# First attention of a two-layer transformer: head outputs closed up by transfers and their sums inverted once per half batch, instead of transposed on TensorE

## The reference

```
q, k, v = split(lora_linear(xn, ...))          # 16 heads of 16
attn = softmax(q k^T / 4)                      # per head, 1024 x 1024
s = lora_linear(concat_heads(attn v), Wo, ...)
x = x + s * g
...
quantize(w) = clip(round(w / (mean|w| + 1e-8)), -1, 1)
hidden = sigmoid(xn quantize(w1)^T) * (xn quantize(w2)^T)   # 704 wide
g = silu(hidden quantize(w3)^T)
```

## Time and profile before

| what | us |
|---|---|
| median of 3 runs | 3152.13 (3145.29 to 3154.65) |
| the profiled execution, its own time | 3151.62 |
| its span in the trace | 3149.8 |
| TensorE busy | 3008.4 (96%) |
| VectorE busy | 2125.9 (67%) |
| ScalarE busy | 1862.8 (59%) |
| first attention, from its first matmul to its last addition | 678.6 to 1450.2 |
| gate network, its first hidden matmul | 1471.3 |

### The profile page before, as it was taken

The page is one execution under the profiler, slowest core; times in us unless marked ns, Lnnn a source line. Parts: engine busy times, 40 slices in busy tenths (PEclk is TensorE's granted clock), DMA queues, the critical chain, the costliest instruction groups (busy, mean ns, idle before and its releaser), DMA issues. The chain is left out here.

```text
span 3149.8 us, 66397 instructions
## 1 busy us (share of the span) xinstructions
PE 3008.4 (96%) x23634; PEld 2263.1 (72%) x23634; DVE 2125.9 (67%) x5893; ACT 1862.8 (59%) x4638; POOL 994.0 (32%) x1611
## 2 busy tenths in 40 slices
PE   7999999999999999996988999999999999999998
PEld 5888888854444444434877888788887888788886
DVE  5666666679989999875755555655556555565556
ACT  4666666647877778783445555455554555545553
POOL 0000000000000000002016666576655766566663
PEclk9999999989999999998999999999999999999999
DMA  4111111232233133102324444354343443244432
GB/s 150 48 48 48 48 48 41 61 69 37 58 50 70 29 75 47 29 9 86 132 67 107 103 97 95 99 126 103 87 114 88 116 103 93 66 116 109 102 87 69
DMA packets 296708, 246.35 MB, mean 78 GB/s; under 512 B 149181, under 2 KB 231741, under 8 KB 296253
## 3 DMA queue, kind: packets, MB, share of 16 engines
q1 hardware_dynamic: 296380, 242.11, 31.6%
HBM read 100.71 MB, written 44.04 MB: 46 GB/s over the span
## 5 line engine op out<-in xcount | busy, mean ns | idle before, releaser
L1821 ACT ACTIVATE b_pp<-b_pp,b_nm 128x192 f32<-128x192 f32 (+2 forms) x1024 | 472.9, 463 | 447.7 <-DVE b_nm L1988 366.2
L973 ACT ACTIVATE a_pt<-ps 128x512 f32<-128x512 f32 x1024 | 555.9, 595 | 177.7 <-PE ps L1005 176.7
L176 DVE TENSOR_REDUCE mx<-ps 128x2 f32<-128x1024 f32 x512 | 622.5, 1224 | 55.5 <-PE ps L167 41.8
L1791 POOL TENSOR_SCALAR b_pp<-b_pp,b_rc 128x192 f32<-128x192 f32 x960 | 387.0, 425 | 386.3 <-DVE b_rc L1997 386.3
L2009 DVE COPY b_pt<-ps 128x384 f32<-128x384 f32 (+2 forms) x336 | 182.1, 556 | 317.9 <-PE ps L1910 302.6
L1988 DVE CUSTOM_DVE_ANT_0 b_pp<-ps,b_mk 128x192 f32<-128x192 f32 x960 | 276.3, 353 | 134.3 <-PE ps L1889 134.3
L800 DVE SCALAR_TENSOR_TENSOR f_yac<-ps,f_cw,f_yac 128x128 f32<-128x128 f32 x992 | 278.0, 344 | 125.4 <-PE ps L599 123.0
L958 POOL TENSOR_TENSOR a_s<-a_s,g 128x256 f32<-128x256 f32 x32 | 23.3, 729 | 880.6 <-DVE a_s L1069 880.6
L599 PEld LDWEIGHTS ps<-w,f_sq 128*128 128x128 f32 x2048 | 265.1, 191 | 26.5 <-issue 6.0
L599 PE MATMUL ps<-w,f_sq 128*128 128x128 f32 x2048 | 270.1, 275 | 0.3
L1944 PE MATMUL ps<-b_wo,b_oT 128*128 128x256 f32 x1024 | 241.6, 380 | 3.7 <-ACT b_vv L1814 3.7
(11 more groups left out here) (273 smaller groups left out, 7313.6 us busy)
## 6 DMA issues: line engine op xcount, KB each, us to landing
b_rt<-b_qf SPq DMA_DIRECT2D x1024, 64.0 KB, 2.0
qk_parts<-f_aa SPq DMA_DIRECT2D x32, 512.0 KB, 2.7
v_rows<-f_va_ SPq DMA_DIRECT2D x16, 512.0 KB, 2.8
rl<-in_W1qT SPq DMA_DIRECT2D x64, 128.0 KB, 2.6
rl<-in_W1kT SPq DMA_DIRECT2D x64, 128.0 KB, 2.7
rl<-in_W1vT SPq DMA_DIRECT2D x32, 256.0 KB, 3.3
b_wo<-in_W1oT SPq DMA_DIRECT2D x16, 512.0 KB, 4.0
b_vs<-b_vv SPq DMA_DIRECT2D x60, 128.0 KB, 2.8
```

The lines of the kernel that those rows point to most:

```text
L176: e.tensor_reduce(M["mx"][kh % 3][:, :, jt, h], P.pair(s), AX.X, ALU.max, negate=True).then_inc(P.free_sem(s), 1)
L973: e.activation(pt[(4 * i + 2 * j + a) % 12][:, :], P.ap((*s, a)), ACT.Exp).then_inc(P.free_sem((*s, a)), 1)
L1791: m = e.tensor_scalar(x, x, r[:, 2 * u + h:2 * u + h + 1], 1.0, ALU.mult, ALU.mult)
L1821: e.activation(x, x, ACT.Exp, bias=nm[n % 4][:, c:c + 1], scale=-1.0, accum_out=sm[n % 4][:, c:c + 1]).then_inc(exp_done, 1)
```

## The change

In the first attention the steps "one" and "two" are gone. After each evacuation SyncE sends eight transfers from SBUF to SBUF: for each of the 4 heads its 16 rows into a tile `oc` without gaps (line 977 of the new program), and its row of sums, folded to 8 rows of 64, into a tile `sm` (line 979). So all sums of a half batch (16 heads, 512 queries) stand in one 128 x 64 tile. Seven side steps per half batch follow: "invert", one reciprocal on VectorE; "spread", SyncE writes it to DRAM (line 983); "return", 16 transfers read it back, each head's row to 16 partitions (line 988); "x", two loads of 256 tokens (992); "norm", POOL multiplies `oc` in place in two parts; and "three" twice, now 256 tokens each, with four matmuls straight from `oc` (line 1097). Side steps still go to chunks 2 to 5; in the last half unit to chunks 1 to 7. The absolute sum and the rounding of w1 and w2 move from the gate network into units 1 and 2 of the first attention (load on SyncE, line 960; absolute sum on ScalarE; matmul; rounding in three passes on POOL). The rounding of w3 moves behind the first hidden step of the second chunk, and the memsets of that block go from VectorE to POOL.

```diff
+GATE = [(s, m, 16 + 20 * m + at) for m in range(2) for s, at in (("load", 0), ("size", 6), ("sum", 8), ("round", 9))]
...
+        p += [("weights", s, m) for s, m, at in GATE if at == i]
...
-        if 2 <= c <= 5 and side:
-            p.append(side.pop(0))
+        if side and (2 <= c <= 5 or c and i >= 16 * units - 8):
+            p += side.pop(0)
         p += ahead(2 * i + 2)
...
-                    p += side
-                    side = [("last",)]
-                f0 = 8 * (u // 4) + 4 * h
-                for n in range(6):
-                    side += [(s, f0 + n - lag) for lag, s in ((2, "three"), (1, "two"), (0, "one")) if 0 <= n - lag < 4]
-    return p + side
+                    p += [s for x in side for s in x]
+                    side = [[("last",)]]
+                f = u // 4 * 2 + h
+                side += [[("invert", f)], [("spread", f)], [("return", f)], [("x", 2 * f), ("x", 2 * f + 1)],
+                         [("norm", f)], [("three", 2 * f)], [("three", 2 * f + 1)]]
+    return p + [s for x in side for s in x]
 
...
+                elif s[:2] == ("weights", "load"):
+                    w.wait_ge(rounded, 3 * n)
+                    w.wait_ge(gate_set, 2)
+                    e.dma_start(raw[:, :, :], A[("f1T", "f2T")[n]].rearrange("(c p) o -> p c o",
+                                                                               p=128)).then_inc(raw_in, 16)
...
-                elif k == "one":
-                    w.wait_ge(x1_ready, n - 2)
-                    e.dma_start(xb[n % 3][:, :], A["x"][n * 128:(n + 1) * 128, :]).then_inc(xb_in[n % 3], 16)
+                elif k == "evac":
+                    b, g, h = n // 8, n // 2 % 4, n % 2
+                    x, f = op[n % 4], 2 * b + h
+                    w.wait_ge(*P.emptied(("group", n)))
+                    if f >= 4:
+                        w.wait_ge(*P.filled(("three", 2 * (f - 4) + 1)))
+                    for j in range(4):
+                        r = 64 * (g % 2) + 16 * j
+                        e.dma_start(oc[f % 4][r:r + 16, g // 2, :], x[32 * j:32 * j + 16, :]).then_inc(closed[n % 4], 16)
+                        r = 32 * g + 8 * j
+                        e.dma_start(sm[f % 4][r:r + 8, :], x[32 * j + 16:32 * j + 17, :].rearrange(
+                            "a (t q) -> a t q", q=64)).then_inc(closed[n % 4], 16)
+                elif k == "spread":
+                    w.wait_ge(rc_ready, n + 1)
+                    e.dma_start(X["inv"][n].rearrange("h (t q) -> (h t) q", q=64), rc[n % 2][:, :]).then_inc(rc_out, 16)
+                elif k == "return":
+                    w.wait_ge(rc_out, 16 * (n + 1))
+                    w.wait_ge(normed, 2 * n)
+                    for i in range(H0):
+                        e.dma_start(rb[i % 8 * 16:i % 8 * 16 + 16, i // 8, :],
+                                    X["inv"][n, i, :].partition_broadcast(16)).then_inc(rb_in, 16)
+                elif k == "x":
+                    w.wait_ge(x1_ready, n - 1)
+                    e.dma_start(xb[n % 2][:, :, :], A["x"][n * 256:(n + 1) * 256, :].rearrange(
+                        "(i p) d -> p i d", p=128)).then_inc(xb_in[n % 2], 16)
...
+                if k == "norm":
+                    w.wait_ge(rb_in, 256 * (n + 1))
+                    for g in (2, 3):
+                        w.wait_ge(*is_closed(8 * (n // 2) + 2 * g + n % 2))
+                    for m in range(2):
+                        x = oc[n % 4][:, :, 256 * m:256 * m + 256]
+                        e.tensor_tensor(x, x, rb[:, :, 256 * m:256 * m + 256], ALU.mult).then_inc(normed, 1)
...
+                elif s[:2] == ("weights", "size"):
+                    w.wait_ge(raw_in, 16 * (n + 1))
+                    e.activation(M["fq"][n][:, :, 0:FF], raw[:, :, :], ACT.Abs,
+                                 accum_out=size[:, n:n + 1]).then_inc(size_ready, 1)
                 elif k == "evac":
-                    u, h = n // 2, n % 2
-                    b, g = u // 4, u % 4
                     w.wait_ge(pv_done, pv_at[8 * n + 7, 1])
-                    if b >= 2:
-                        w.wait_ge(*P.filled(("one", 8 * (b - 2) + 7)))
-                    e.activation(oT[b % 2][:, g, h * CH:(h + 1) * CH], P.ap(("group", n)),
-                                 ACT.Copy).then_inc(P.free_sem(("group", n)), 1)
+                    if n >= 4:
+                        w.wait_ge(*is_closed(n - 4))
+                    e.activation(op[n % 4][:, :], P.ap(("group", n)), ACT.Copy).then_inc(P.free_sem(("group", n)), 1)
...
-                elif k == "one":
-                    b, t = n // 8, n % 8
-                    w.wait_ge(*P.emptied(("group", 2 * (4 * b + 3) + t // 4)))
-                    for g in range(4):
-                        m = e.transpose(P.ap(s)[:, g * 128:(g + 1) * 128], oT[b % 2][:, g, t * 128:(t + 1) * 128],
-                                        ident[:, :])
-                    m.then_inc(P.full_sem(s), 1)
-                elif k == "two":
-                    w.wait_ge(*P.emptied(("one", n)))
+                elif s[:2] == ("weights", "sum"):
+                    w.wait_ge(size_ready, n + 1)
+                    e.matmul(P.ap(s)[:, 0:3], ones[:, :], size[:, :], start=True, stop=True).then_inc(P.full_sem(s), 1)
+                elif k == "three":
+                    w.wait_ge(normed, n + 1)
                     for i in range(2):
-                        m = e.transpose(P.ap(s)[:, i * 128:(i + 1) * 128], av[n % 2][:, i * 128:(i + 1) * 128],
-                                        ident[:, :])
-                    m.then_inc(P.full_sem(s), 1)
-                elif k == "three":
-                    w.wait_ge(*P.emptied(("two", n)))
-                    for i in range(2):
-                        m = e.matmul(P.ap(s)[:, 0:256], aT[n % 2][:, i, :], M["wo"][:, i, :], start=i == 0,
-                                     stop=i == 1)
+                        t = slice(256 * (n % 2) + 128 * i, 256 * (n % 2) + 128 * i + 128)
+                        for j in range(2):
+                            m = e.matmul(P.ap(s)[:, i * 256:(i + 1) * 256], oc[n // 2 % 4][:, j, t], M["wo"][:, j, :],
+                                         start=j == 0, stop=j == 1)
...
-                elif k == "one":
-                    p = P.ap(s).rearrange("p (h r) -> p h r", r=32)
+                elif s[:2] == ("weights", "sum"):
                     w.wait_ge(*P.filled(s))
+                    e.tensor_scalar(thr[:, 0, n:n + 1], P.ap(s)[:, n:n + 1], 1.0 / (FF * D), 1e-8, ALU.mult,
+                                    ALU.add).then_inc(P.free_sem(s), 1)
+                elif k == "invert":
+                    for g in (2, 3):
+                        w.wait_ge(*is_closed(8 * (n // 2) + 2 * g + n % 2))
                     if n >= 2:
-                        w.wait_ge(*P.filled(("two", n - 2)))
-                    e.reciprocal(rc[n % 2][:, :], p[:, :, 16]).then_inc(rc_ready, 1)
-                    w.wait_ge(rc_ready, n + 1)
-                    e.tensor_tensor(av[n % 2][:, :].rearrange("p (h d) -> p h d", d=16), p[:, :, 0:16],
-                                    spread(rc[n % 2][:, :], 2, 16), ALU.mult).then_inc(P.free_sem(s), 1)
-                elif k == "two":
-                    w.wait_ge(*P.filled(s))
-                    if n >= 2:
-                        w.wait_ge(*P.filled(("three", n - 2)))
-                    e.tensor_copy(aT[n % 2][:, :, :],
-                                  P.ap(s)[:, 0:256].rearrange("p (k t) -> p k t", k=2)).then_inc(P.free_sem(s), 1)
+                        w.wait_ge(rc_out, 16 * (n - 1))
+                    e.reciprocal(rc[n % 2][:, :], sm[n % 4][:, :]).then_inc(rc_ready, 1)
                 elif k == "three":
                     w.wait_ge(*P.filled(s))
                     w.wait_ge(s2_ready, n - 1)
-                    e.tensor_tensor(s1[n % 2][:, :], P.ap(s)[:, 0:256], M["bob"][:, :],
-                                    ALU.add).then_inc(P.free_sem(s), 1)
+                    e.tensor_tensor(s1[n % 2][:, :, :], P.ap(s).rearrange("p (i d) -> p i d", d=256),
+                                    spread(M["bob"][:, :], 1, 2), ALU.add).then_inc(P.free_sem(s), 1)
...
-    p = [(f, order[0]) for f in front.values()] + [("quantize",)]
+    p = [(f, order[0]) for f in front.values()]
...
+            if (i, n) == (1, 0):
+                p.append(("quantize",))
```

145 lines of the change are left out of this document (72 added, 73 removed).

## The result

| | before | after |
|---|---|---|
| median of the runs | 3151.4 us (4 runs) | 3226.3 us (3210.2 to 3244.5, 4 runs) |
| ratio | | 1.0248, 95% interval 1.0216 to 1.0280 |
| profiled execution, its span | 3151.6, 3149.8 | 3244.5, 3242.7 |

What follows compares the result with a forecast made beforehand. TensorE, busy 96% of the span, was taken as the bound, with VectorE close; -25.9 transposes, +49.9 lateness, +52.2 clock, +11.6 last half unit, +15.4 tail, -9.2 gate weights, +2.5 ScalarE make +96.5 on 3151.6: 3248 us, range 3152 to 3290.

Steps and rivals of the forecast that it cites:

- transposes: First attention's loop: 24 side steps lose their transposes on TensorE, -25.9 us.
- stops of units 2, 6, 10, weight block in: Ends of first halves: rows queue behind 26 late loads, 6.5 us each, +19.5; a weight block ahead of unit 2's rows.
- all other lateness in the loop: Rows late behind 18 loads, a weight block, or the returns in the other units: 27.4 us.
- clock and restart behind these three stops: Second halves of units 2, 6, 10: each stop brings 37.5 us at half clock, 17.4 us lost each, +52.2.
- last half unit: First attention's end: TensorE stops 7.7 us for the product, then two projections and half clock: +11.6 us.
- tail: Last evacuation to last addition: closing chain starts anew, projections at half clock, 32.9 us for 17.5: +15.4.
- front of the network, third weight: Gate network: rounding leaves its front, -12.2; third weight in second chunk costs TensorE some 3 (0 to 6): -9.2 together.
- ScalarE's passes: Units 1 and 2: two passes on ScalarE and two small matmuls for the gate weights, +2.5 us (0 to 4).
- Rival 1: Clock behind the three stops falls but comes back soon (3.4 us): clock term 5, total 3201 us; chance 0.27.
- Rows are not late: Rival: rows pass the loads or SyncE issues faster; lateness and clock terms go, 3146 us, no change; chance 0.10.
- VectorE sets the pace: Rival: VectorE's queue holds the half unit, projections vanish under it, -42.3 for -25.9, 3130 us; chance 0.10.
- More falls of the clock: Rival: the stop of unit 1 and those of 3.5 us bring the clock down too, 3288 us; chance 0.08.

Runs made afterwards that it cites:

- the two profiles of the change: The changed kernel profiled in the run at 3244.5 us, then run once more unchanged for a second profile: median 3219.4 us of those 4 runs.
- returns in two: Against loads first: the 16 returns made 2 transfers, third weight summed beside the first hidden steps, 5 tiny loads added; 3144.9 us, ratio to before 0.9978.
- gate weights alone: Kernel before with only the change's handling of the three gate-network weights; transposes, outputs and side work as before: 3150.5 us, ratio 1.0013.
- 30 small loads: Kernel before with 30 small loads ahead of the rows of the second halves of units 2, 6 and 10; three stops, 24.1 us: 3177.3 us, ratio 1.0094.
- loads first: Changed kernel, but SyncE issues the loads of the unit after next and a weight block ahead of the closing transfers: 3172.1 us, ratio to before 1.0066.
- closings on GpSimd: Changed kernel, but GpSimd instead of SyncE issues the 8 closing transfers behind each evacuation: 3177.0 us, ratio to before 1.0071.
- 14 loads: Kernel before with 14 small loads ahead of the rows of the second halves of units 2, 6 and 10: median 3154.2 us of ten runs.
- fewer closings: Against returns in two: the four transfers of sums of a half unit issued as one, 5 closings for 8; 3136.7 us, ratio to before 0.9967.
- fewer closings with 62 tiny matmuls: Against fewer closings: 62 tiny matmuls added where TensorE waits for the last half batch's product; 3138.3 us, ratio to before 0.9962.
- the two padded kernels: Kernel before plus 66 tiny matmuls ahead of the last side step's transposes, 3172.5 us; and fewer closings with 62 tiny matmuls, 3138.3 us.

## Why the prediction was right, and where it was not

| term | forecast | measured, in the two profiles of the change where nothing else is said |
|---|---|---|
| transposes | -25.9 | -8.9 in a batch with rows in time (136.9 for 145.8, returns in two), so -27 |
| stops of units 2, 6, 10, weight block in | 22.5 | 23.0 and 22.7 |
| all other lateness in the loop | 27.4 | 10.5 and 14.9 of waits |
| clock and restart behind these three stops | 52.2 | 21.4 and 11.5 |
| what is left of the loop, half clock elsewhere above all | 0 | 32 and 13 |
| last half unit | +11.6 | +8.1 and +6.9 |
| tail | +15.4 | +11.1 and +11.1 |
| front of the network, third weight | -12.2, +3 | -12.8, +7.3 |
| ScalarE's passes | +2.5 | +5.0 (gate weights alone) |
| second attention | 0 | +14.0 and +10.4 |

The row of what is left is the loop's +73.6 and +47.0 less the rows above it, the last half unit and ScalarE's passes, so it is no measurement of its own.

**The mechanism was right.** The closings tie SyncE to the evacuation, the loads start late, the rows queue up behind them in issue and in landing, and TensorE stops ahead of the score: 25.0 us after the evacuation by the working, 25.2 in unit 6. The issues have the size taken from transfers of another kind (0.54 and 0.65 us where 0.66 was taken). For the half units behind the returns the same arithmetic gave too much: 18 us forecast, 12.0 regained with two returns. With those returns 16 issues in 7.27 us became 2 in 1.28.

**The step that failed is the clock's price.** That each of the three stops brings the clock down was my estimate from the earlier trace rows; each did, and the granted clock then stood at 0.50 for 13.7, 10.2 and 44.4 us in the first profile of the change and for 13.7, 20.5 and 6.8 in the second. But I took the one long stretch shown, at this attention's start, for the rule, and priced it at 17.4 us; the half units of 35.1 lost 13.8 each. Rival 1 described the usual stop; the long stretch is a chance, which one profile had twice (37.5 us behind a stop of 1.1, 44.4 in one of 6.9), and the other not at all. With the 7 us of the longer stops in place of 52.2, my sum would be 3203, below all eight runs. What closed the gap to 3226 were things I hadn't in it: half clock elsewhere in the loop (13 to 32 us) and the second attention (10 to 14), against 12 to 17 us of lateness too many. So the nearness of 3248 to 3226 is in good part luck. As a share of the span the clock behind the stops is small in the run with the longer stops, 7 of 3182 us with the restarts. In the first profile of the change the two half units of 35.1 alone lost 27.6 of 3243 us, and by the table some 50 us of its loop go to the clock and restarts, over 1.5%.

**Third weight.** I took 3 us, with TensorE a step or two ahead. TensorE's matmul for the sum waits for VectorE's reduction, which stands in VectorE's queue behind its work on the hidden steps, and TensorE's later matmuls stand behind that matmul: 7.2 us. VectorE's queue, not its passes, was the size to take.

**Tail and last half unit.** At 28.6 the tail has the forecast form; its last projections (8 matmuls, 16 records) took 5.3 us, not 9: they run from 1524.92 to 1530.22, and the granted clock came back from 0.50 to 1.00 at 1528.18. In the last half unit the two projections cost what was forecast (22.7 without a stop or a fall of the clock, returns in two, for 17.9 + 4.5). The stop forecast at 7.7 us was 3.5 in one profile and absent in the other, where 20.5 us of half clock slowed TensorE instead. So +8.1 is near +11.6 for another reason than the one given.

**Range.** Its lower end, from the numbers given for it, is 3151 (3201 - 38 - 12), not 3152.

**Rivals.** Rows are not late: no. VectorE sets the pace: no, half units with two projections take 25.3 us, as in the forecast (near 26), even with rows in time. More falls of the clock: yes in number, most of them short.

## What to carry to other kernels

When a change puts a transfer that waits on an event into a queue, list what stands behind it there: here one reordering of SyncE's queue was worth some 50 us, more than anything the change saved. Ask of each new batch of small transfers whether one descriptor pattern can do it (16 into 2, 4 into 1); only then did fewer transposes turn into time. And price a stop by several executions, since what the clock does behind it differs from run to run.

## What the runs showed of the hardware

- In the loops of six profiles (the two of the changed kernel, loads first, closings on GpSimd, 14 and 30 small loads) the granted clock fell 29 times with a stop of TensorE of 1.0 us or more in the 10 us ahead or in progress. It then stood at 0.50 for 3.4 to 20.5 us in 26 cases and for 37.5, 41.0 and 44.4 in three, and differently with the same program: 10.2 us in unit 6 in one profile of the changed kernel, 20.5 in the other. The 41.0 us came with the stop of 2.6 (14 loads), a loss of 13.8 us in the profiled run; five of the ten runs of that kernel lost nothing to be seen in their times.
- It also fell with no stop of over 0.9 us ahead: in the last half unit of the first attention for 20.5 us in three profiles (the first of the changed kernel, loads first, fewer closings), and not at all there in two others (returns in two, fewer closings with 62 tiny matmuls).
- A closing took GpSimd 0.51 to 0.52 us to issue, and SyncE 0.54 (rows of outputs) and 0.65 (row of sums). With them on GpSimd its first instruction of the gate network came 4.25 us after its last addition, for 0.31 with the loads first.
- The 66 and 62 float32 matmuls with 2 columns of the two padded kernels stand as 132 and 124 records. The 66 took 24.96 us, 0.38 each, with their weight loads busy for 24.87 us of it and a mean granted clock of 0.57.
- Packets of the instruction queue (16 KB) came once per 123.7 matmul records in the kernel before and per 123.4 after the change, in the mean. Of SyncE's issues in the second attention of the changed kernel within 1.5 us of one, 27% took 0.9 to 2.1 us, with a median of 0.59 over all issues; of the others under 1% took over 0.85.
